# By-key scores in three split passes, statistics behind the maxima in step 0, and two residual biases a step later

## What is computed

```
x = x + tanh(g_xattn) * attention(layernorm(x), ctx)      # q, k, v, o projections, softmax over 120 keys
h = layernorm(x)
x_scale = max(amax(|h|), 1e-6) / 127 ; h_q = clip(round(h / x_scale))
x = x + tanh(g_ffn) * ((h_q @ weight_q.T) * x_scale * weight_scale + bias)
```

## Time and profile before

| What | Value |
|---|---|
| Median of three runs | 840.54 us |
| Profiled execution | 840.9 us, its span 839.1 us |
| PE busy | 819.8 us, 98% |
| DVE busy | 533.9 us, 64% |
| ACT busy | 514.2 us, 61% |
| POOL busy | 508.2 us, 61% |
| Mean granted TensorE clock | 0.999 |
| One odd step (i = 5) and one even step (i = 6) | 50.00 us and 51.07 us |

### The profile page before, as it was taken

One profiled execution on the slowest core, in us unless ns is written; L12 is line 12 of the kernel. 1 busy time (PEld: TensorE's weight loads), 2 busy tenths in 40 slices (PEclk: granted clock), 3 DMA queues, 4 the chain that ended last, 5 costly groups with the idle time before them and its releaser, 6 DMA issues.

```text
span 839.1 us, 16066 instructions
## 1 busy us (share of the span) xinstructions
PE 819.8 (98%) x6318; PEld 513.9 (61%) x6318; DVE 533.9 (64%) x758; ACT 514.2 (61%) x714; POOL 508.2 (61%) x514
## 2 busy tenths in 40 slices
PE   9999999999999999999999999999999999999996
PEld 6655666666666656666666656656666656655563
DVE  4865657666566766558566566756658655555568
ACT  4665466566665666566566665566566665665675
POOL 3535475664758557385673757557485664665587
PEclk9999999999999999999999999999999999999999
DMA  8531614132231522314232241421414122111112
GB/s 290 202 104 48 194 31 159 52 129 78 64 126 52 157 76 45 120 54 156 74 107 74 78 139 51 131 84 57 126 51 143 60 66 73 39 51 52 51 51 100
DMA packets 39626, 79.62 MB, mean 95 GB/s; under 512 B 6912, under 2 KB 8320, under 8 KB 37504
## 3 DMA queue, kind: packets, MB, share of 16 engines
q1 hardware_dynamic: 38976, 77.75, 28.9%
q10 hardware_dynamic: 576, 0.85, 0.3%
HBM read 61.78 MB, written 16.81 MB: 94 GB/s over the span
## 4 chain that ended last, share of the span: by engine, by line
PE 73%; DVE 17%; issue 3%; POOL 3%; ACT 2%; DMA 1%; DVEq 0%; SPq 0%; POOLq 0%; ACTq 0%
PE bank_b L326 21%; PE bank_a L326 13%; PE scores L372 8%; PE pv_ps L400 7%; PE sum_ps L402 6%; PE scores L386 5%; DVE row_max L1055 5%; DVE xt_lo L1045 5%; PE bank_a L446 3%; DVE u_sb L1135 2%; PE bank_a L355 2%; PE bank_b L355 2%; PE scores L326 1%; PE scores L390 1%; POOL x L1366 1%
## 5 line engine op out<-in xcount | busy, mean ns | idle before, releaser
L1055 DVE TENSOR_REDUCE row_max<-scores 128x16 f32<-128x1920 f32 x64 | 138.1, 2158 | 120.0 <-PE scores L372 120.0
L1379 POOL TENSOR_TENSOR x<-x,u_sb 128x512 f32<-128x512 f32 x56 | 75.6, 1350 | 159.4 <-DVE u_sb L1135 157.2
L746 ACT ACTIVATE probs<-scores 120x2048 f32<-120x2048 f32 x64 | 120.3, 1880 | 64.2 <-PE scores L390 63.9
L1370 POOL TENSOR_TENSOR o_lo<-on,o_hi 128x512 fp32r<-128x512 f32 x63 | 86.7, 1378 | 74.8 <-ACT o_hi L762 74.1
L1045 DVE TENSOR_TENSOR xt_lo<-xt,xt_hi 128x512 fp32r<-128x512 f32 x64 | 65.3, 1046 | 64.7 <-ACT xt_hi L705 64.7
L1374 POOL TENSOR_TENSOR x<-x,gbias_r 128x512 f32<-128x512 f32 x64 | 82.0, 1282 | 37.6 <-ACT cen L768 36.6
L372 PEld LDWEIGHTS scores<-k_sb,q_sb 32*128 32x128 f32 x2048 | 62.9, 186 | 52.8 <-issue 52.3
L1336 POOL TENSOR_TENSOR xt<-xt,rstd_b 128x512 f32<-128x512 f32 x60 | 92.3, 1563 | 4.3 <-ACT rstd_b L990 2.9
L1366 POOL TENSOR_TENSOR x<-x,gbo_r 128x512 f32<-128x512 f32 x64 | 88.4, 1392 | 3.3 <-DMA x<-in_x 3.2
L762 ACT ACTIVATE o_hi<-on 128x512 fp32r<-128x512 f32 x64 | 40.4, 632 | 73.3 <-DVE on L1068 73.2
L386 PE MATMUL scores<-q_sb,k_sb 32*120 32x512 f32 x512 | 72.6, 636 | 4.0 <-DVE row_max L1055 3.1
(11 more groups left out here) (183 smaller groups left out, 1784.1 us busy)
## 6 DMA issues: line engine op xcount, KB each, us to landing
xt<-in_x_t SPq DMA_DIRECT2D x16, 1024.0 KB, 5.4
x<-in_x SPq DMA_DIRECT2D x64, 256.0 KB, 3.0
out_x<-x SPq DMA_DIRECT2D x61, 256.0 KB, 2.1
x_in<-in_x SPq DMA_DIRECT2D x60, 256.0 KB, 3.7
rstd_b<-rstd_rows SPq DMA_DIRECT2D x14, 256.0 KB, 4.7
ctx_sb<-in_ctx_t SPq DMA_DIRECT2D x8, 360.0 KB, 4.8
probs<-in_wq SPq DMA_DIRECT2D x4, 256.0 KB, 3.7
x<-in_wo SPq DMA_DIRECT2D x1, 1024.0 KB, 9.3
```

The lines of the kernel that those rows point to most:

```text
L746: act.activation(probs[0:KEYS], scores[0:KEYS], ACT.Exp, scale=SCALE).then_inc(p_ready, 1)
L1055: dve.tensor_reduce(row_max[:].rearrange("p (t r) j -> p r t j", r=ROWG)[:, :, :, j], scores[:, :, 0:QT * KEYS].rearrange("p r (t k) -> p ...
L1370: pool.tensor_tensor(o_lo[i % 2][:, j], on[:, j % 2], o_hi[i % 2][:, j].bitcast(F32), ALU.subtract).then_inc(o_split, 1)
```

## The change

Three things change. First, `scores_by_key` no longer multiplies float32 operands: for each slot ACT copies `q_sb` and `k_sb` to float32r (`split_high`, two instructions), DVE subtracts (`split_low`, two instructions), and PE makes three passes of four float32r matmuls in place of four float32 products. PE waits for `qk_split` ahead of them. There are two buffers for each half, used by j modulo 2, so `split_high(i, j)` waits for the by-key scores two slots earlier. Second, in step 0 DVE's statistics of batch 3 and `gate_rows` stand behind the maxima of their slots, and at the end of every step `dequantise(m, 1)` stands ahead of `x1_statistics(m, 3)`. Third, POOL's `bias_x(i, 2)` and `bias_x(i, 3)` move from the end of step i to slot 0 or 1 of step i + 1. In the last step two `normalise_o` and the biases are reordered too.

```diff
             def scores_by_key(i, j):
-                for r in range(ROWG):
-                    pe.matmul(scores[0:KEYS, r], k_sb[i // 2 % 2][STRIPS[r], j, keys_of(i)], q_sb[STRIPS[r], j],
-                              start=True, stop=False)
+                pe.wait_ge(qk_split, nth(i, 2 * DT, 2 * j + 1))
+                q, k = (q_hi[j % 2], q_lo[j % 2]), (k_hi[j % 2], k_lo[j % 2])
+                for p, (a, b) in enumerate(((0, 0), (0, 1), (1, 0))):
+                    for r in range(ROWG):
+                        pe.matmul(scores[0:KEYS, r], k[a][STRIPS[r]], q[b][STRIPS[r]], start=p == 0, stop=False)
...
+            def split_high(i, j):
+                act.wait_ge(q_ready, nth(i, DT, j))
+                act.wait_ge(k_ready, nth(i // 2, DT, j))
+                if i > 0 or j >= 2:
+                    act.wait_ge(s_done, nth(i, DT, j) - 2)
+                act.activation(q_hi[j % 2][:], q_sb[:, j], ACT.Copy).then_inc(qk_hi_done, 1)
+                act.activation(k_hi[j % 2][:], k_sb[i // 2 % 2][:, j, keys_of(i)], ACT.Copy).then_inc(qk_hi_done, 1)
...
+            def split_low(i, j):
+                dve.wait_ge(qk_hi_done, nth(i, 2 * DT, 2 * j))
+                dve.tensor_tensor(q_lo[j % 2][:], q_sb[:, j], q_hi[j % 2][:].bitcast(F32), ALU.subtract).then_inc(qk_split, 1)
+                dve.wait_ge(qk_hi_done, nth(i, 2 * DT, 2 * j + 1))
+                dve.tensor_tensor(k_lo[j % 2][:], k_sb[i // 2 % 2][:, j, keys_of(i)], k_hi[j % 2][:].bitcast(F32),
+                                  ALU.subtract).then_inc(qk_split, 1)
```

ACT, in `step` and `last_step`:

```diff
                 if is_batch(b):
                     bias_q(b, 0, bank_a)
+                split_high(i, 1)
                 log_sums(i, 0)
                 invert_sums(i, 0)
+                split_high(i, 2)
...
                 log_sums(i, 1)
                 invert_sums(i, 1)
+                split_high(i, 3)
...
                 log_sums(i, 2)
                 invert_sums(i, 2)
+                if is_batch(b):
+                    split_high(b, 0)
...
                 exponentials(i, 1)
                 high_o(i, 0)
+                split_high(i, 2)
                 integers(e, 2)
                 integers(e, 3)
...
                 copy_zt(e, 1, bank_a)
+                split_high(i, 3)
                 centre(m, 1)
```

DVE, in `step` and `last_step`:

```diff
                 if i > 0 and is_batch(f):
                     x_statistics(f, 0)
+                split_low(i, 1)
                 if is_batch(e):
                     quant_max(e, 2)
                     quant_max(e, 3)
...
                 normalise_o(i, 0)
                 if i == 0:
+                    split_low(i, 2)
                     low_ctx(pair)
                     x_statistics(2, 2)
                     x_statistics(2, 3)
-                    x_statistics(3, 0)
...
-                if is_batch(f):
+                if i > 0 and is_batch(f):
                     x_statistics(f, 1)
+                if i > 0:
+                    split_low(i, 2)
                 if is_batch(b):
                     maxima(b, 1)
                 normalise_o(i, 1)
+                if i == 0:
+                    x_statistics(3, 0)
+                    x_statistics(3, 1)
...
-                if is_batch(f):
+                if i > 0 and is_batch(f):
                     x_statistics(f, 2)
-                if i == 0:
-                    gate_rows()
+                split_low(i, 3)
...
                 normalise_o(i, 2)
+                if i == 0:
+                    x_statistics(3, 2)
+                    gate_rows()
...
                     x_statistics(f, 3)
+                if is_batch(b):
+                    split_low(b, 0)
...
                 if is_batch(m):
+                    dequantise(m, 1, sum_ps)
                     x1_statistics(m, 3)
-                    dequantise(m, 1, sum_ps)
...
                 x1_statistics(m, 1)
                 normalise_o(i, 1)
                 quant_max(m, 0)
+                split_low(i, 3)
                 quant_max(m, 1)
                 quant_factors(m, 0)
```

POOL:

```diff
                 if is_batch(m):
                     bias_x1(m, 0)
+                    bias_x(m, 2)
+                    bias_x(m, 3)
...
                     bias_x(i, 0)
                     bias_x(i, 1)
-                bias_x(i, 2)
-                bias_x(i, 3)
...
                 bias_x1(m, 0)
                 x1_deviations(m, 0)
+                bias_x(m, 2)
+                bias_x(m, 3)
                 bias_x(i, 0)
```

More of the change, by code:

```diff
@@ L80, in gated_layer @@
         q_sb = sb("q_sb", [P, DT, S])
+        q_hi, q_lo = ([sb(f"q_{part}{i}", [P, S], F32R) for i in range(2)] for part in ("hi", "lo"))
+        k_hi, k_lo = ([sb(f"k_{part}{i}", [P, KEYS], F32R) for i in range(2)] for part in ("hi", "lo"))
         k_sb = [sb(f"k_sb{i}", [P, DT, KEYS2]) for i in range(2)]
@@ L131, in gated_layer @@
         q_done, q_ready = sem("q_done"), sem("q_ready")
+        qk_hi_done, qk_split = sem("qk_hi_done"), sem("qk_split")
         v_done, v_ready = sem("v_done"), sem("v_ready")
@@ L981, in _ @@
             bias_q0(1)
+            split_high(0, 0)
             for c in range(1, CT):
@@ L1224, in last_step @@
                 quant_factors(e, 1)
+                normalise_o(i, 0)
                 residual(m, 0, bank_a)
                 x1_statistics(m, 0)
-                normalise_o(i, 0)
+                split_low(i, 2)
                 residual(m, 1, bank_b)
@@ L1296, in _ @@
             maxima(0, 1)
+            split_low(0, 0)
             x_statistics(1, 3)
```

## The result

The changed kernel takes 845.93 us (median of seven executions, 844.72 to 849.86), the kernel before 840.72 (839.98 to 841.07): a ratio of 1.0078, with an interval of 1.0063 to 1.0094. (The ratio goes by all executions, the three long ones too; that of the two medians is 1.0062.) It is slower by 5.2 us, where 837.0 was forecast.

A forecast was written before the change was run, and what follows sets the result against it. PE was taken to bound the kernel. Terms of -2.2, -0.7, -3.7, +0.6 and +2.5 sum to -3.5 us, from the profiled 840.9 to 837.4, and 837.0 as median; range 828 to 842.

The forecast's parts named there:

- The passes: By-key scores on PE: three float32r rounds save 0.17 us a slot, at most 10.9 us over 64 slots.
- the loads do not hide: Rival: weight loads do not overlap the round before, +0.34 us a slot, 861 us in all; chance 0.04.
- DVE and POOL alternate: Slot 0 of middle steps: q_lo and k_lo each wait out a POOL addition, taking about 1.5 us each.
- an odd step: Middle steps: PE waits some 0.9 us for the maxima ahead of slot 1, and the step gains nothing.
- The splits slip through: Rival: k_lo or q_lo gets ahead of POOL in slot 0, so maxima are not late; 828 us, chance 0.27.
- Even steps: Steps 2 to 12: slot 1 starts 0.1 us earlier, each step gains 0.6, six give -3.7 us.
- What stands behind `maxima(b, 0)` is late too: Slot 0: exponentials(i, 1), up to 1.1 us later on ACT, still lies under the 12 matmuls of project_q(b, 1).
- Step 14: Its 1.41 us wait at slot 1 grows by 1.1, slots 1 to 3 return 0.5: +0.6 us.
- Prologue and step 0: Prologue's split delays one maxima by 0.4 us without effect; step 0 loses its 1.43 wait and gives -2.2 us.
- Last step: ACT and DVE set the pace; the splits delay dequantise(e, 2) by about 2 us: +2.5, bounds 0.5 and 3.5.
- the maxima come later still: Rival: q_lo, k_lo and q_unit each wait out POOL, maxima(b, 0) another 1.2 us later; 843 us, chance 0.11.

The follow-up runs named there:

- passes alone: The changed kernel with its splits run only for batch 0, slots 0 and 1, PE's work complete, other scores wrong: 824.35 us, ratio 0.9816.
- Units first: The changed kernel with POOL's quant_units(e, 1) before bias_x1(e, 3) in slot 0 of each step: 832.25 us, ratio 0.9903.
- Keys first: The changed kernel with ACT's bias_k(pair, 0) before quant_round(e, 2) and (e, 3) in slot 0 of even steps: 849.04 us, ratio 1.0106.
- four moves: The changed kernel with units first, keys first, prologue's split later, and last-step splits earlier with low_o before bias_x: 830.72 us, ratio 0.9874.
- Five moves: Four moves plus ACT's bias_k(pair, 1) ahead of high_o(i, 0) in slot 0 of even steps: 823.93 us, ratio 0.9800.
- the filler: The changed kernel with twelve unread bf16 matmuls on PE ahead of the maxima wait in slot 1 of step 14: 845.15 us, ratio 1.0053.
- orders alone: The kernel before with only the change's reordering of DVE and POOL, and no splits: 833.03 us, ratio 0.9911.
- prologue's split later: The changed kernel with DVE's split_low(0, 0) behind maxima(0, 2) instead of maxima(0, 1): 846.53 us, ratio 1.0073.

## Why the prediction was wrong

- **The passes (right).** Rounds end 0.23 apart, loads hide, and the passes alone are worth 8.7 to 10.3 us against 10.9 forecast. The rival "the loads do not hide" is refuted: it needed rounds of 0.41. The rule of the Trainium skill on row groups ("TensorE: Matmul & The Clock Gate", Part 3, What overlaps and what doesn't), which stood beside it, is not what these rounds show.
- **DVE and POOL alternate (right).** `q_lo` 1.64 and `k_lo` 1.37 us, maxima at 12.9 after the step's start where 13.0 was forecast, and an odd step that gains 0.13, forecast nothing. Units first shows the cause: with POOL's addition out of the way, odd steps fall by 0.84. "The splits slip through" was the state to be had by design, not by luck.
- **Even steps (wrong, 7.7 us, most of the error).** The median missed the forecast by 8.9 us. The profiled span missed it by 12.1: 7.7 here, 2.8 in step 14, 2.3 in the prologue and step 0, less 0.7 in the rest. The step that failed is that of step 6: "the maxima come 13.0 after it, so an even step starts slot 1 0.1 earlier". It took the maxima for all that is late on DVE, and asked only whether they come before PE. The same chain also holds `q_rec`, on which ACT's rounding waits, and behind the rounding the bias that empties PE's bank for `project_k`. PE never reached slot 1 at 13.12 or earlier, but waited 1.46 us ahead of it and started it 14.17 after the step's start. The sentence "What stands behind `maxima(b, 0)` is late too" followed only `exponentials`. Keys first and four moves show that there is a third way as well, the second bias behind `high_o`. Five moves cuts all three, and the even step falls from 51.74 to 49.76.
- **Step 14 (mis-sized).** The wait was right (2.87 for 2.5), its price wasn't: forecast +0.6, measured +3.4 in the profiled execution. The difference is TensorE's clock after the wait: where it stays up, with the filler and also in keys first without one, the step takes 47.66 and 47.6, which is +0.5 and +0.4. The prediction had no term for the clock.
- **Prologue and step 0 (partly wrong).** Step 0's wait of 1.43 is gone, and orders alone gives 2.0 in that step, forecast 2.2. But "nothing comes of it" was said of the prologue's split, and the profile has +1.8 there, 1.3 of it because DVE's `max_sp` lost to a POOL instruction that started at the same time. Step 0 then gave 1.7 of its 2.2, with the low clock at its start. What an average execution loses by it stays open, and so does what brings the two starts together.
- **Last step (right).** +2.4 for +2.5. PE waits 0.67 for `k_lo` and 1.43 for `u_sb`; four moves takes both away.
- **The rival on the slower side** ("the maxima come later still") had the right sign and the wrong mechanism: in the middle steps nothing came later than forecast, but more things were waited for. Its sum was too low as well: 1.2 us in twelve steps and step 14 are 15.6, not 10, so half of it with the last step at +3.5 gives 846, not 843. That figure lies on the measured time by luck, since what it assumes did not happen.

The order alone was not seen as a gain of its own. The forecast folded it into the slots, where the splits used it up: the passes alone lie 15.9 us below the kernel before on their chip (840.26 and 824.35), the splits took 21.6 as they were placed, and next to nothing as placed in five moves (823.93). Five moves also shifts other work that passes alone leaves in place, so this last figure is for the whole arrangement, not for the splits by themselves.

## What to carry to other kernels

When work is put ahead of a late instruction, list every semaphore that the delayed engine raises from there on and follow each to the engine that bounds the kernel, through queues of third engines too; the small waits already in the list of waits (2.7 us in six times here) name the next ones. A two-operand instruction on VectorE should not meet a running addition on GpSimd: put on GpSimd, at that place, something that itself waits for VectorE, and the split of 120 columns costs 0.27 us and not 1.37. Measure the cost of a change and of its placement apart, by a kernel that leaves the added work out.

## What the runs showed of the hardware that was not expected

- TensorE's clock can go from 2.4 to 1.2 GHz after short idle times: after 2.87 us (changed kernel) and after 1.79 us, there 0.6 us after the work had begun again (five moves). In the changed kernel it stayed low for nearly all of the 12 matmuls behind it (5.03 for 2.98 us), and cost 2.9 us in step 14. Nearly the same wait doesn't always bring it: with slot 1 of step 14 waiting 2.84 to 2.87 us, that step took 50.56 us (changed kernel), 49.23 (prologue's split later) and 47.6 (keys first, clock at 1.00); with 1.74 to 1.79 us it took 48.1 (four moves, five moves) and 46.6 (units first, clock at 1.00). What decides it, these profiles don't show. The 1.46 us of waiting in each even step of the changed kernel were not followed by it in its profile. In keys first, waits of 0.41 and 1.44 us within 3 us were, in two of six even steps, which took 53.3 us in place of 51.75. Window of step 6 there, slots 0 and 1, with a granted clock of 0.89:

```profile
334.00:350.00 16.00, 14.15 (x112) 10.12 (x108) 10.26 (x16) 10.42 (x19) 8.30 (x10) 0.89 0.45 155
```

- Which of VectorE and GpSimd gets through when they start almost together turns on hundredths of a microsecond. A VectorE instruction recorded at 37.15 against GpSimd's 37.14 took 1.59 us. The filler's kernel had the two at 36.64 and 36.66 and took 0.23. But with units first it started at 36.66 against 36.68, ahead by the record, and still took 1.61. The Trainium skill ("SBUF — State Buffer", SBUF: two separate sides) says that whichever starts first keeps the other out for its whole instruction; the first two pairs agree. The third would only if the recorded starts were uncertain by some 0.02 us, which no run here shows.
